# Moving the absolute-sum pass of the ternary weights from the attention stage to the layer norm and QKV stages

## The reference, cut to what matters

```python
x = x + LN(attn0(LN(x)))          # causal attention, S=2048, D=1024, value convolution
x = x + LN(ffn0(LN(x)))           # ternary weights
...
def attn0(x):
    q, k, v = split(x @ W_qkv + b_qkv)
    A = softmax(mask(q @ k.T / sqrt(d)))
    C = w0 * v_prev + w1 * v + w2 * v_next
    return A @ C - diag(A)[:, None] * (w2 * v_next)

def ternary(w):
    scale = max(mean(abs(w)), 1e-8)
    return clip(round(w / scale), -1, 1)

def ffn0(x):
    h = gelu(x @ ternary(W1).T + b1)      # W1: 4096 x 1024
    return h @ ternary(W2).T + b2         # W2: 1024 x 4096
```

## Time and profile before

| | us |
|---|---|
| median of 2 runs | 6266.33 |
| lowest, highest | 6252.63, 6280.03 |
| profiled execution, its own time | 6120.12 |
| its span (slowest core) | 6118.2 |
| spans of the eight cores | 6078.8 to 6118.2 |

### The profile page before, as it was taken

How to read it: one execution, slowest core, us unless ns; L and a number is a source line. 1 busy time by engine, 2 the same in 40 slices (tenths; PEclk the granted TensorE clock), 3 DMA queues, 4 the chain that set the end, 5 groups by cost and what they waited for, 6 DMA issues and landing times.

```text
span 6118.2 us, 42482 instructions; the slowest of 8 cores (6078.8 to 6118.2 us)
## 1 busy us (share of the span) xinstructions
PE 2877.8 (47%) x11532; PEld 1141.4 (19%) x11532; DVE 1930.2 (32%) x4826; ACT 905.3 (15%) x924; POOL 369.9 (6%) x298
## 2 busy tenths in 40 slices
PE   0672421121666665661352020664351189889870
PEld 0221100010212121210110020221111033333330
DVE  4225333346000000003546552232335322222234
ACT  0003700000213030302000001001100132232220
POOL 2000000001000000001101310000001000000001
PEclk9995655555767575755665555776575599999995
DMA  1102533411443434340001003000000221111103
GB/s 28 28 14 90 162 89 86 88 36 55 85 95 69 93 72 90 71 86 7 0 0 49 7 1 35 7 0 0 14 0 1 34 48 30 28 28 28 28 4 106
DMA packets 501887, 274.46 MB, mean 45 GB/s; under 512 B 441216, under 2 KB 449440, under 8 KB 501664
## 3 DMA queue, kind: packets, MB, share of 16 engines
q1 hardware_dynamic: 437248, 201.40, 13.9%
q0 software_dynamic: 64416, 70.34, 7.1%
HBM read 190.97 MB, written 33.55 MB: 37 GB/s over the span
## 4 chain that ended last, share of the span: by engine, by line
PE 39%; DVE 21%; DMA 15%; issue 11%; ACT 7%; POOL 5%; SPq 2%; DVEq 1%; POOLq 0%; ACTq 0%
DMA w2tb<-w2t_sc 7%; POOL sq_scr L208 4%; PE ps_m5a L2333 4%; PE ps_m5b L2333 4%; PE ps_o L1048 4%; PE ps_i5a L2294 4%; PE ps_i5b L2294 4%; PE ps_qkv L441 3%; DVE lnst L214 3%; PE ps_h L1000 3%; DMA w1t_sc<-wtb 2%; DMA w2t_sc<-wtb 2%; SPq L982 2%; DVE n1e L1979 1%; PE ps_q L1994 1%
## 5 line engine op out<-in xcount | busy, mean ns | idle before, releaser
L1048 PE MATMUL ps_o<-w2tb,h_g 128*128 128x512 bf16 x1024 | 436.7, 580 | 291.3 <-DMA w2tb<-w2t_sc 260.5
L1000 PE MATMUL ps_h<-act_fm,w1tb 128*128 128x512 bf16 x1024 | 282.2, 425 | 156.6 <-ACT h_g L1018 81.6
L2333 PE MATMUL ps_m5a<-w2b,scaled 128*128 128x512 bf16 x1024 | 262.1, 402 | 111.4 <-DVE scaled L2316 111.2
L2306 ACT ACT_TABLE_LOAD x128 | 164.2, 1283 | 771.8 <-PE ps_i5a L2294 699.2
L2333 PE MATMUL ps_m5b<-w2b,scaled 128*128 128x512 bf16 x1024 | 259.1, 399 | 0.0
L1083 DVE TENSOR_REDUCE smB<-out2g 128x1 f32<-128x1024 bf16 x16 | 19.5, 1220 | 724.6 <-ACT out2g L1071 724.6
L2294 PE MATMUL ps_i5a<-act_fm,w1b 128*128 128x512 bf16 x1024 | 233.4, 381 | 27.1 <-DMA w2b<-L_ffn_w 27.1
L2316 DVE TENSOR_TENSOR scaled<-scaled,rw2b_eg 128x512 bf16<-128x512 bf16 x256 | 97.4, 421 | 448.9 <-ACT scaled L2306 448.9
L2294 PE MATMUL ps_i5b<-act_fm,w1b 128*128 128x512 bf16 x1024 | 231.5, 379 | 0.0
L208 POOL TENSOR_TENSOR sq_scr<-X 128x1024 f32<-128x1024 f32 x96 | 181.6, 1892 | 776.7 <-issue 494.3
L1048 PEld LDWEIGHTS ps_o<-w2tb,h_g 128*128 128x128 bf16 x1024 | 110.1, 123 | 615.8 <-issue 606.6
(11 more groups left out here) (314 smaller groups left out, 4302.7 us busy)
## 6 DMA issues: line engine op xcount, KB each, us to landing
tw<-L_ffn_W SPq DMA_DIRECT2D x128, 512.0 KB, 4.6
w1b<-L_ffn_w POOLq DMA_DIRECT2D x8, 2048.0 KB, 13.4
w2b<-L_ffn_w POOLq DMA_DIRECT2D x8, 2048.0 KB, 22.6
w1t_sc<-wtb POOLq DMA_DIRECT2D x32, 256.0 KB, 4.8
w2t_sc<-wtb POOLq DMA_DIRECT2D x32, 256.0 KB, 5.2
xt<-L_attn_x SPq DMA_DIRECT2D x16, 512.0 KB, 4.0
x_sc<-X SPq DMA_DIRECT2D x16, 512.0 KB, 2.6
xt<-x_sc SPq DMA_DIRECT2D x16, 512.0 KB, 4.1
```

Source lines behind the costliest of these rows:

```text
L1000: t.matmul(pb[:, half * 512:(half + 1) * 512], w1tb[:, slot * 4096 + kc * 512 + fl * 128: slot * 4096 + kc * 512 + (fl + 1) * 128], act_fm ...
L1048: ins = t.matmul(ps_o2[u][:, half * 512:(half + 1) * 512], h_g[:, fc * 512 + sub * 128:fc * 512 + (sub + 1) * 128], wslice[:, half * 512:( ...
L2306: cs.inc(s.activation(scaled[:, ipr * 1024:(ipr + 1) * 1024], ps_i5[bk][:], AF.Gelu))
L2333: ins = t.matmul(ps_m5[bk][:], scaled[:, ic * 512 + u * 128:ic * 512 + (u + 1) * 128], w2b[:, slot * 8192 + ic * 1024 + half * 512: slot * ...
```

## The change

The code that defines the passes moves ahead of the layer norm. Pass 1 has its own list, b0p1_steps, its own loads into two slots, tw1, and its own scratch output, absd, both in the region that C_tm takes later. Two steps are popped ahead of each tile's stats in the layer norm (32 steps), and in QKV one per block of 128 output columns in groups 0 to 3 and two in groups 4 and 5 (32 steps). b0_steps now holds tau_step, the six first loads and pass 2. Attention pops 3 entries in tile 0 and 6 in every other tile. Two small constants are set at the start of the program.

```diff
+        tw = kb.at("tw", [128, NSLOT * 1024], F32, REG1)
+        NSLOT1 = 2
+        tw1 = kb.at("tw1", [128, NSLOT1 * 1024], F32, REG5)
+        absd = kb.at("absd", [128, 1024], BF16, REG5 + NSLOT1 * 4096)
...
+        def mk_pass1(src_ap, col):
+            load = {}
+            slot = col % NSLOT1
+
+            def prefetch():
+                twa = tw1[:, slot * 1024:(slot + 1) * 1024]
+
+                def _(sync, w=b0_state["p1_free"][slot], ds=dts1[slot]):
+                    wait(sync, w)
+                    ds.inc(sync.dma_start(
+                        out=twa.rearrange("p (c d) -> p c d", c=src_ap.shape[1]),
+                        in_=src_ap))
+                kb.q(_)
+                load["twa"], load["tok"] = twa, dts1[slot].tok()
+
+            def step():
+                def _(s, ltok=load["tok"], twa=load["twa"],
+                      pv=b0_state["abs_prev"]):
+                    wait(s, ltok, pv)
+                    cs.inc(s.activation(absd[:], twa, AF.Abs,
+                                        accum_out=asums[:, col:col + 1]))
+                kb.s(_)
+                b0_state["abs_prev"] = cs.tok()
+                b0_state["p1_free"][slot] = cs.tok()
+            return prefetch, step
...
         for i in range(NT):
+            for _k in range(2):
+                if b0p1_steps:
+                    b0p1_steps.pop(0)()
             stok = lnb.stats(xstage[:, i * D:(i + 1) * D], i, [xload], prev=stok)
         rtok = lnb.rstd_batch(0, 16, [stok])
...
             for fc4 in range(4):
+                if b0p1_steps:
+                    b0p1_steps.pop(0)()
+                if grp >= 4 and b0p1_steps:
+                    b0p1_steps.pop(0)()
...
-            for _k in range(9 if i else 4):
+            while b0p1_steps:
+                b0p1_steps.pop(0)()
+            for _k in range(6 if i else 3):
                 if b0_steps:
                     b0_steps.pop(0)()
```

More of the change, by code:

```diff
@@ L385, in build @@
[L385 to L508, removed]
@@ L535, in build @@
         dts = [kb.dsem("t%d" % k) for k in range(NSLOT)]
+        dts1 = [kb.dsem("u%d" % k) for k in range(NSLOT1)]
         dst_sem = kb.dsem("ts")
@@ L545, in build @@
         b0_state.update(slot_free={k: None for k in range(NSLOT)},
+                        p1_free={k: None for k in range(NSLOT1)},
                         abs_prev=None, g_prev=None, st_tok=None, tau_tok=None)
@@ L552, in _ @@
             def _(sync, w=b0_state["slot_free"][slot], ds=dts[slot],
-                  w2=(reg1_free if col < NSLOT else None)):
+                  w2=(b0_state.get("reg1_free") if col < NSLOT else None)):
                 wait(sync, w, w2)
@@ L682, in build @@
         _p2 = [mk_pass2(s_, c_) for s_, c_ in batches]
-        for k in range(NSLOT):
+        b0p1_steps = []
+        for k in range(NSLOT1):
             _p1[k][0]()
@@ L700, in build @@
         b0_steps.append(_pf2_initial)
-        for k in range(32):
+        for k in range(64):
             def mk(k=k):
@@ L708, in build @@
             b0_steps.append(mk())
[L709 to L717 removed]
+    q_fm = kb.at("q_fm", [128, ND * T], BF16, REG2)
+    k_fm = kb.at("k_fm", [128, ND * T], BF16, REG3)
+    v_fm = kb.at("v_fm", [128, ND * T], BF16, REG4)
@@ new lines, in build, with _ @@
+    kb.flush_dbg()
+    kb.barrier()
+    with ExitStack() as pha:
+        wbuf = kb.at("wbuf", [128, 2 * 8 * 512], BF16, WS)
+        ps_q = [kb.psum("ps_qkv0", [128, 512], F32, pha),
+                kb.psum("ps_qkv1", [128, 512], F32, pha)]
+        Wq = inp["L0_attn_W_qkv"].rearrange("(c p) f -> p c f", p=128)
+        dws = [kb.dsem("w0"), kb.dsem("w1")]
+        slot_tok = {0: None, 1: None}
+        bank_tok = {0: None, 1: None}
+        for grp in range(6):
+            slot = grp % 2
+            def _(g, grp=grp, slot=slot, w=slot_tok[slot], ds=dws[slot]):
+                wait(g, w)
+                ds.inc(g.dma_start(
+                    out=wbuf[:, slot * 4096:(slot + 1) * 4096].rearrange(
+                        "p (c f) -> p c f", c=8),
+                    in_=Wq[:, :, grp * 512:(grp + 1) * 512]))
+            kb.g(_)
+            wtok = dws[slot].tok()
+            for fc4 in range(4):
+                if b0p1_steps:
+                    b0p1_steps.pop(0)()
+                if grp >= 4 and b0p1_steps:
+                    b0p1_steps.pop(0)()
+                fc = grp * 4 + fc4
+                mat, lc = fc // 8, fc % 8
+                dst = (q_fm, k_fm, v_fm)[mat]
+                bk = fc4 % 2
+                pb = ps_q[bk]
+                for tg in range(4):
+                    def _(t, pb=pb, slot=slot, fc4=fc4, tg=tg, wtok=wtok,
+                          fc=fc, w=bank_tok[bk]):
+                        wait(t, wtok, w)
+                        for kc in range(8):
+                            t.matmul(pb[:],
+                                     wbuf[:, slot * 4096 + kc * 512 + fc4 * 128:
+                                          slot * 4096 + kc * 512 + (fc4 + 1) * 128],
+                                     n1_fm[:, kc * T + tg * 512: kc * T + (tg + 1) * 512],
+                                     start=(kc == 0), stop=False)
+                        ct.inc(t.matmul(pb[:], bqkv_row[0:1, fc * 128:(fc + 1) * 128],
+                                        ones_b[0:1, :], start=False, stop=True))
+                    kb.t(_)
+                    mtok = ct.tok()
+                    def _(v, pb=pb, mat=mat, lc=lc, dst=dst, tg=tg, mtok=mtok):
+                        wait(v, mtok)
+                        dd = dst[:, lc * T + tg * 512: lc * T + (tg + 1) * 512]
+                        if mat == 0:
+                            cv.inc(v.tensor_scalar_mul(dd, pb[:], 1.0 / 32.0))
+                        else:
+                            cv.inc(v.tensor_copy(dd, pb[:]))
+                    kb.v(_)
+                    bank_tok[bk] = cv.tok()
+            slot_tok[slot] = cv.tok()
+        qkv_done = cv.tok()
+        b0_state["reg1_free"] = qkv_done
+        kb.dbg("q_fm", q_fm[:], qkv_done)
+        kb.dbg("k_fm", k_fm[:], qkv_done)
+        kb.dbg("v_fm", v_fm[:], qkv_done)
@@ new lines, in build, with _ @@
+    kb.flush_dbg()
+    kb.barrier()
+    with ExitStack() as pha:
+        cbuf = kb.at("cbuf", [128, T], BF16, WS)
+        ps_trc = kb.psum("ps_trc", [128, 1024], BF16, pha)
+        ev = None
+        ttk = None
+        for c in range(ND):
+            vchunk = v_fm[:, c * T:(c + 1) * T]
+            w0 = wv_pp[:, c * 3 + 0:c * 3 + 1]
+            w1 = wv_pp[:, c * 3 + 1:c * 3 + 2]
+            w2 = wv_pp[:, c * 3 + 2:c * 3 + 3]
+            def _(v, vchunk=vchunk, w1=w1, ev=ev):
+                wait(v, ev, pro_dg, qkv_done)
+                cv.inc(v.tensor_scalar_mul(cbuf[:], vchunk, w1))
+            kb.v(_)
+            t1 = cv.tok()
+            def _(v, vchunk=vchunk, w0=w0, t1=t1):
+                wait(v, t1)
+                cv.inc(v.scalar_tensor_tensor(cbuf[:, 1:T], vchunk[:, 0:T - 1], w0,
+                                              cbuf[:, 1:T], ALU.mult, ALU.add))
+            kb.v(_)
+            t2 = cv.tok()
+            def _(v, vchunk=vchunk, w2=w2, t2=t2):
+                wait(v, t2)
+                cv.inc(v.scalar_tensor_tensor(cbuf[:, 0:T - 1], vchunk[:, 1:T], w2,
+                                              cbuf[:, 0:T - 1], ALU.mult, ALU.add))
+            kb.v(_)
+            t3 = cv.tok()
+            for half in range(2):
+                ev, ttk = transpose_tile(
+                    kb, lambda j, half=half: cbuf[:, half * 1024 + j * 128:
+                                                  half * 1024 + (j + 1) * 128],
+                    8, ps_trc[:],
+                    lambda j, c=c, half=half: C_tm[:, (half * 8 + j) * D + c * 128:
+                                                   (half * 8 + j) * D + (c + 1) * 128],
+                    idbf[:], [t3, gid], ps_free=ev)
+        c_done = ev
+        kb.dbg("C_tm", C_tm[:], c_done)
```

68 lines of the change are left out of this document (34 added, 34 removed).

## The result

| | kernel before | changed kernel |
|---|---|---|
| median of all runs, us | 6134.26 (12 runs) | 6080.1 (13 runs) |
| ratio, 95% interval | | 0.9913 (0.9878 to 0.9948) |
| span of the profiled execution, slowest core | 6118.2 | 6082.0 |

The changed kernel is 0.87% faster, 53 us of 6134 (32 to 75). That is less than 2%, but the interval excludes 1. Of the runs of either kernel a few were disturbed on one die; they stand in the medians and are left out of the ratio, and the two that were known ahead of time, 6252.63 and 6280.03, lie over 2% above the fastest, as such runs do.

The account below looks back on a forecast made before the run. Attention was taken as bound by ScalarE's queue in tiles 0 to 7, then by the single buffer wtb's store waits. Attention -60, layer norm +23 and first QKV weights +3 gave -34: 6266.33 - 34 = 6232 us, range 6075 to 6265.

Parts of the forecast that it names:

- the footing: Whole kernel: time put on the two-run median 6266.33, giving 6232, not on the profiled 6120.12, giving 6086 (chance 0.15).
- Layer norm, +23: Ahead of QKV: 32 sums and their loads delay the logarithm from 107 to 130 us, +23 (13 to 40).
- the step after x: Layer norm, once x has landed: the remaining 23 sum steps take 3.6 us each, 83 us in all.
- Rival 3: Layer norm: loads slip in beside x, steps take 3.0 us, +13 there; whole -60, 6206 us; chance 0.10.
- the +24: Layer norm: loads get their turn beside x, 14 get in, x ends 24 us later; the sum would be -33.
- First QKV weights, +3: Start of QKV: two sum loads of 1.73 us meet the exposed first weight load, +3 us (0 to 4).
- Attention, -60: Attention, exponential 0 to 15: 720.6 us against 780.3, a gain of 60 us (45 to 74).
- the pitch of W1's stores: Attention's ternary steps: W1 stores land 6.6 us apart against 7.2 for W2; 25 of them cost 165.0 us.
- The 52 waits: Attention: spread ternary steps pay 52 store pitches in place of some 55, 349.8 us in all.
- The lost cover in tiles 12 to 14: Attention's tiles 12 to 14: no ternary step hides TensorE's next scores, 3 x 5.6 = 16.8 us more.
- Rival 1: Layer norm: the ring of two slots is too short, a slot turn doubles to 14.4 us; 6315 us, chance 0.08.
- Rival 2: Whole kernel: nothing left, with layer norm +40, weight load +4 and attention -45, so -1, 6265 us; chance 0.12.

Follow-up runs that it names:

- four per tile: The changed kernel with pass 2 spread over all 16 attention tiles, 4 entries popped in most tiles and 5 in tiles 1 and 2: ratio 0.9891 to the kernel before.
- the control: The kernel before, run again with no edit: ratio 1.0001 (0.9966 to 1.0035).
- two buffers on the kernel before: The kernel before with wtb as two bf16 store buffers, each with its own semaphore, and nothing else changed: ratio 0.9642 to the kernel before.

## Why the prediction was right or wrong

It said within 2% and -34 us on a sum of -60 + 23 + 3. Measured are 53 us (32 to 75) by timing, and 34 us at the first add after attention by the marks.

**The step that failed** is the last one, from the sum to the forecast. The gain of 34 us was put on the median of two runs, 6266.33, and taken for no change, since two per cent "is 125 us, about what a measurement of this kernel can tell from no change". The runs showed 6134.26 for the kernel before, and an interval of 0.35% to either side of the ratio, in which a gain of 0.87% is plain. Of the 152 us between the forecast 6232 and the measured 6080.1, 132 are the footing and 20 the size of the change.

In the sum itself the mechanism and the sign of each term were right, and two sizes were not. That it agrees with the marks (-34) is partly luck: the layer norm was put 10 us too dear, attention's gain 8 us too large and the first weights 1 us too cheap.

- **Layer norm, +23.** Measured +12.8, just under the lower bound of 13. The end of x was right (45.9 where 47 was said), and so was the guess for a step beside x (5.7 us where 5.3 was said). The term mis-sized is the step after x: 3.6 us, from a load that takes 4.5 us. The loads took 3.6 us in the median, so the step is 3.1, and 22 of them give 11 us less. The load of the earlier trace rows was not alone, as the prediction read it: two loads of 512 KB were issued and 1.06 MB moved from 1377 to 1383.5. Rival 3 had a step of 3.0 and +13 for this part.
- The Trainium skill ("DMA: Bandwidth & Descriptors", section on queues, rings and completion order) lets a DMA engine take turns between its queues, a whole packet at a time. The trace agrees in part: the loads got their turns and x paid, 11.5 us for about 7 loads of 1.73 us, and with four slots it ended at 61 us. But the loads were slowed too, 5.7 us a step against 3.1, so the +24 that the prediction took from this rule did not come.
- **First QKV weights, +3.** Measured +4.4 (17.2 - 12.8), just over the bound of 4.
- **Attention, -60.** Measured -52, inside 45 to 74. Mis-sized is the pitch of W1's stores, 6.6 us. It was read in tile 8 of the kernel before, its first full tile of stores, and the longer pitch of later tiles was taken for a trait of W2. After the change the 26 waits for W1 cost 123.8 us and the 26 for W2 124.2. W1's stores lay 7.0 us apart in the mean of tiles 1 to 5, and over 7 in tiles 4 and 5, which was named as a sign of being wrong. The trace of before showed it already: in its tile 10, W1's stores, seven apart in the chain of waits, give 6.9 us each:

```profile
916.43 4.74 DMA w1t_sc<-wtb
...
965.07 5.24 DMA w1t_sc<-wtb
```

- **Attention, the rest.** Why the pitch grows with the tile stays open. The 52 waits came out right; at 4.8 us each and 2.2 of work they are 364 us, not 350, 14 us more. The lost cover in tiles 12 to 14 was real and rightly priced: they take 101.4 us on core 5 where 99.9 were said, and with four per tile the waits behind TensorE's scores fall from 29.5 to 7.1 us.
- **The footing.** The range reached the other footing, but the point did not. Ten more runs showed that the first two were not typical. The profiled execution was the right base: from 6120.12 the sum gave 6086, and the median is 6080.1.
- **Within 2%, 0.93.** True as a bound, but the 0.55% should have been forecast as a gain.

Rival 1, the short ring, did not come: after the end of x a turn of a slot took 6.2 us, far from 10.2 (only beside x did it take 11 to 12). Rival 2 did not come either. Of the 19 us between -53 by timing and -34 by the marks, 10 stand in a feed-forward stage that did not change; that they are chance is argued from the control, not proved, and -34 lies inside the interval of the timing.

## What to carry to other kernels

Where a short periodic wait stands in an in-order queue, count how many of its turns fall behind other work: here each tile hides the first, so the same 64 steps cost least when they are spread evenly. By the first add the spreading was worth 21 to 31 us and moving the other work 4 to 14, by which was done first. Before work is moved to an idle engine, look at what its loads will meet: ScalarE was idle in two stages, but in one the DMA engines were at 0.94 while x was loaded and in the other at 0.12, and only the second was free, once its first weights had landed. And ask what the wait is for: a second buffer in the same bytes, by a narrower type, gave 3.6% by itself where this change gave 0.9%.

## What the runs showed of the hardware

- More loads in flight can make the whole later: four slots in place of two moved the end of x from 45.9 us (core 5) to 61.1 (core 3) and the logarithm from 120.8 to 133.6 in the mean.
- A store of the same 256 KB of bf16 lands sooner from a bf16 source: 4.1 to 4.3 us against 5.2 to 5.3 from f32, which is twice the bytes read and a conversion; the loads beside it fell from 4.5 to 4.0.
- A table load of 1283 ns stands before each of the absolute sums even where they follow one another in ScalarE's queue with only a branch between them.
- The granted clock differs between pairs of cores in one execution. QKV, the same matrix products everywhere, took 279 to 281 us at 1.00 (2.4 GHz) on most cores; with two buffers on the kernel before it took 295 at 0.93 on cores 0 and 1 and 307 to 308 at 0.87 on cores 4 and 5. In the mean of eight cores that is 11 us, so a mark should be read core by core before a difference is put down to an edit.
